# An int4 SwiGLU beside an S4 convolution on one core: each down-weight piece converted one group earlier, and the change of phase laid out anew

## Chip, cores and metric

One Trainium2 chip, one core. The metric is device time of one execution in microseconds (us), smaller is better.

## What is computed

The input is `u`, 2048 rows of 1024 numbers. The reference, cut to its core:

```python
xn = _layernorm(u)
K  = _s4_kernel(...)                       # 1024 taps, from a 64-state S4 system
y  = irfft(rfft(xn, 2L) * rfft(K, 2L))[:L] + D[0] * xn     # causal convolution along the row
Wg, Wu, Wd = dequantize(...)               # 4-bit words, (w - zero) * scale in groups of 64
h  = silu(xn @ Wg.T) * (xn @ Wu.T)         # 2752 columns
out = u + y + h @ Wd.T
```

## The kernel before, in words

Every large product runs with Strassen's scheme in Winograd's form: a 2 by 2 block product is done with seven smaller products (for x and h: A11, A12, S1 to S4, A22; for weights: B11, B21, B22, T1 to T4). Each factor is split into two float16 parts, a high part (rounded by ACT) and a low part (what is left, by GpSimd), and three of the four part products are taken. So each weight or hidden block goes through DVE (dequantize, sums), ACT (high part) and GpSimd (low part).

**Head (0 to 164 us).** x is read, normalized, and turned by TensorE into the stationary copies `xo[0]` and `xo[1]`, seven blocks each. Units 0 and 1 run beside it.

**Phase A.** 44 units; unit n is one tile of 128 hidden columns for gate and up on one half p of the rows, seven products of 12 matmuls in the order `TURN` (0, 3, 2, 1, 4, 5, 6). Between products ACT takes copies of the banks (`snap_s1`, `snap_s5`, `snap_u2`, `snap_u3`), on which the next products of the same unit wait (`products`, `snap_done`). Units 2 and 3 are written out; then the loop over groups g = 1 to 9 has units 4g to 4g+3. Unit 40 and the two short units 41 and 42 (64 columns left over, `tail_products`) end the phase with unit 43, which TensorE runs last.

In the same loop the down weight is prepared: piece g (`down_nibble`, `down_words`, `d_high`, `d_sum`, `d_low`) is 256 rows of it. In the kernel before, group g handles piece g-1, and its last four sums come in group g+1. Piece 8's sums lie beside unit 40, and piece 9 comes after the last, short piece 10, in the change of phase. Finished pieces are stored to `w_d` (`store_w`) from the slots `ds` and `ds_more`; hidden blocks are stored to `h_d` (`store_h`).

Words, scales and zeros of a weight tile come as a slab (`load_slab`, two slots `raw`/`sz`): 256 KB of words and 512 KB of scales and zeros. Slab m may be issued once slab m-2 is dequantized (`deq_done` at m-1).

**Phase B.** 56 down products, (sp_, j, s) in order, 33 matmuls each (`down`), with `wd[j]` (2816 KB each, read back from `w_d`) as moving and `hr` (704 KB for each product) as stationary data. DVE adds each to `acc`. 48 convolution pieces of 12 matmuls (`conv`) stand between them by the table `conv_pieces`; their strips come from two matmuls with `flip` after product (0, 0, 1), which need `kshift` from DRAM. The normalized x for them is stored to `xc_d` (8 blocks of 1024 KB, `store_xc`) and read back (`load_xc`).

**What sets the order.** Each engine's program is written out by hand. SP issues nearly all DMAs, and a wait in SP's program holds everything behind it. ACT issues only the first parts of `wd[0]`, `wd[1]` and `wd[2]` (`load_wd` in ACT's program, nine of eleven slices each); SP issues their rest and `wd[3]` to `wd[6]`. In the change of phase ACT's program has `load_wd(0)` behind `silu_tail(41)`, then the first half of piece 9 (`down_nibble(NG - 1, 0)`), `silu_tail(42)`, `load_wd(1)`, and `down_nibble(NG - 1, 1)` ahead of `snap_s1(43)`. A `down_nibble` waits for its slab.

## Time and profile before

| | us |
|---|---|
| three timed runs | 1496.56, 1498.66 (median), 1504.98 |
| the profiled execution | 1495.27 |
| its span in the trace | 1493.5 |
| TensorE busy in the span | 1333.8 (89%) |
| VectorE (DVE) / ScalarE (ACT) / GpSimd (POOL) busy | 957.6 / 457.3 / 674.7 |

The page gives busy time of each engine over the span. A stage view splits the span and shows which engine is full in which stage; a timeline gives for each instruction how long its engine sat idle before it, and who released it. Line numbers are those of the kernel before.

### The profile page before, as it was taken

The page shows a single profiled execution, that of the slowest core. Times are in us where ns is not written, and L with a number is a line of the kernel's source. Part 1 is how long each engine was busy: PE and PEld are TensorE (multiplying, and loading weights), DVE is VectorE, ACT ScalarE, POOL GpSimd, SP SyncE. Part 2 cuts the span into 40 slices and gives each one's busy share as a digit, 9 for nine tenths or more (in the row PEclk, how much of TensorE's full clock was granted, in tenths as well). Part 3 has the DMA queues.
Part 4 walks back from the last instruction along what each step waited for, and adds up shares of the span by engine and source line. Part 5 has one row for each costly group of instructions (what it writes and reads, how often), then busy time and mean ns, then how long its engine had stood idle before and what let it go on. Part 6 is the DMA issues. An engine that isn't in the chain of part 4 may idle for free. (4 is left out here: it accounts for less than half of the span.)

```text
span 1493.5 us, 17048 instructions
## 1 busy us (share of the span) xinstructions
PE 1333.8 (89%) x6299; PEld 630.9 (42%) x6299; DVE 957.6 (64%) x1057; ACT 457.3 (31%) x801; POOL 674.7 (45%) x484
## 2 busy tenths in 40 slices
PE   1557899988998999989999999449999999999998
PEld 1423444433443444434444444124444444444444
DVE  4744478899999898678898988535233332432341
ACT  3533444434444354444444543221000000000000
POOL 3642466766678688687978786341000000000000
PEclk9978999999999999999999999769999999999999
DMA  5301554343433344344444443779756236335431
GB/s 177 86 29 70 225 166 131 125 133 115 132 124 117 131 134 140 124 139 134 142 134 141 139 137 112 233 247 365 248 185 222 92 109 221 92 110 196 126 101 57
DMA packets 164646, 218.09 MB, mean 146 GB/s; under 512 B 41426, under 2 KB 121940, under 8 KB 162644
## 3 DMA queue, kind: packets, MB, share of 16 engines
q1 hardware_dynamic: 163988, 209.86, 42.8%
q10 hardware_dynamic: 576, 7.14, 1.4%
q8 instruction: 50, 0.82, 0.2%
q14 instruction: 32, 0.26, 0.1%
HBM read 139.64 MB, written 77.34 MB: 145 GB/s over the span
## 5 line engine op out<-in xcount | busy, mean ns | idle before, releaser
L1310 PE MATMUL px<-xo,wo 128*128 128x512 f16 x2016 | 473.9, 389 | 59.1 <-ACT py L960 30.2
L1310 PEld LDWEIGHTS px<-xo,wo 128*128 128x128 f16 x2016 | 200.1, 100 | 308.7 <-issue 26.5
L684 POOL TENSOR_TENSOR wo<-wf,wo 128x512 f16<-128x512 f32 x147 | 236.5, 1619 | 71.9 <-ACT wo L918 71.9
L703 POOL TENSOR_TENSOR hs<-hf,hs 128x512 f16<-128x512 f32 x154 | 210.8, 1375 | 103.2 <-ACT hs L953 96.1
L1394 PE MATMUL px<-wd,hr 128*128 128x512 f16 x1056 | 235.0, 382 | 10.7 <-DMA wd<-w_d 10.7
L1310 PE MATMUL pz<-xo,wo 128*128 128x512 f16 x1008 | 233.6, 382 | 0.0
L1394 PEld LDWEIGHTS px<-wd,hr 128*128 128x128 f16 x1056 | 102.6, 98 | 131.1 <-DMA wd<-w_d 11.2
L1310 PEld LDWEIGHTS pz<-xo,wo 128*128 128x128 f16 x1008 | 99.5, 99 | 120.8 <-issue 4.6
L1925 DVE SCALAR_TENSOR_TENSOR acc<-px,acc 128x512 f32<-128x512 f32 x32 | 22.1, 691 | 155.3 <-PE px L1394 151.3
L953 ACT ACTIVATE hs<-hf 128x512 f16<-128x512 f32 x154 | 94.5, 621 | 80.8 <-DVE hf L1569 48.2
L693 POOL TENSOR_TENSOR ds<-wf,ds 128x512 f16<-128x512 f32 x69 | 104.2, 1511 | 33.1 <-ACT ds_more L939 20.1
L1310 PE MATMUL py<-xo,wo 128*128 128x512 f16 x504 | 117.6, 384 | 0.0
L1479 DVE TENSOR_TENSOR wf<-wf,sz 128x1024 f32<-128x1024 int32 x63 | 113.4, 1800 | 5.7 <-ACT wf L893 3.8
L1394 PE MATMUL pz<-wd,hr 128*128 128x512 f16 x528 | 116.6, 379 | 0.0
L1480 DVE SCALAR_TENSOR_TENSOR wf<-wf,sz 128x1024 f32<-128x1024 f32 x63 | 112.6, 1788 | 2.2
L918 ACT ACTIVATE wo<-wf 128x512 f16<-128x512 f32 x147 | 90.8, 621 | 75.8 <-DVE wf L1480 55.4
L708 POOL TENSOR_TENSOR u<-u,s 128x512 f32<-128x512 f32 x42 | 60.6, 1442 | 56.7 <-ACT u L978 56.2
L1394 PEld LDWEIGHTS pz<-wd,hr 128*128 128x128 f16 x528 | 50.9, 98 | 58.6
L1310 PEld LDWEIGHTS py<-xo,wo 128*128 128x128 f16 x504 | 49.9, 99 | 60.7 <-issue 2.8
L1259 ACT ACTIVATE xc<-ctmp 128x512 f16<-128x512 f32 x8 | 5.0, 629 | 218.1 <-DVE ctmp L1950 218.1
L1477 DVE TENSOR_SCALAR wf<-raw 128x512 int32<-128x512 int32 x63 | 59.2, 939 | 17.4 <-DMA sz<-in_sz_down 12.8
L1264 ACT ACTIVATE us<-ctmp 128x512 f16<-128x512 f32 x16 | 10.1, 629 | 190.2 <-DVE ctmp L1970 190.2
(211 smaller groups left out, 1406.5 us busy)
## 6 DMA issues: line engine op xcount, KB each, us to landing
h_d<-hs SPq DMA_DIRECT2D x154, 256.0 KB, 3.7
hr<-h_d SPq DMA_DIRECT2D x56, 704.0 KB, 4.2
w_d<-ds SPq DMA_DIRECT2D x69, 256.0 KB, 3.9
wd<-w_d SPq DMA_DIRECT2D x4, 2816.0 KB, 12.5
sz<-in_sz_gate SPq DMA_DIRECT2D x21, 512.0 KB
sz<-in_sz_up SPq DMA_DIRECT2D x21, 512.0 KB
sz<-in_sz_down SPq DMA_DIRECT2D x20, 512.0 KB
xc_d<-xo SPq DMA_DIRECT2D x8, 1024.0 KB, 10.5
```

Source lines behind the costliest of these rows:

```text
L684: pool.tensor_tensor(w_dest(t, j, 1), w_place_of(j), w_dest(t, j, 0), ALU.subtract).then_inc(wlo_done, 1)
L693: pool.tensor_tensor(d_dest(q)[:, 1, :], d_place_of(g, j), d_dest(q)[:, 0, :], ALU.subtract)\
L703: pool.tensor_tensor(hs[:, j, :, 1, :], h_place_of(p, j), hs[:, j, :, 0, :], ALU.subtract)\
L708: pool.tensor_tensor(u3[:, :], u3[:, :], s5[:, :], ALU.add).then_inc(u2_done, 1)
L918: act.activation(w_dest(t, j, 0), w_place_of(j), ACT.Copy).then_inc(whi_done, 1)
L953: act.activation(hs[:, j, :, 0, :], h_place_of(p, j), ACT.Copy)\
L1310: done = pe.matmul(bank[:, :], wo[t % 2][:, j, wp, k * P:(k + 1) * P], xo[p][:, j, xp, k, :], start=(j in (0, 3) and k == 0 and wp == 0 an ...
L1394: done = pe.matmul(bank[:, :], hr[slot][:, k, hp, :], wd[j][:, k, wp, :], start=(OPENS[j] and k == 0 and hp == 0 and wp == 0), stop=(k == ...
L1477: link(dve.tensor_scalar(q[:, 1, :], r, 15, None, ALU.bitwise_and))
L1479: link(dve.tensor_tensor(w, q, sz[:, slot, 1:2, :].broadcast_to((P, 2, 512)), ALU.subtract))
L1480: dve.scalar_tensor_tensor(out=w, in0=w, scalar=WS, in1=sz[:, slot, 0:1, :].broadcast_to((P, 2, 512)), op0=ALU.mult, op1=ALU.mult).then_in ...
L1925: dve.scalar_tensor_tensor(out=part, in0=banks[BANK[j]][s][:, :], scalar=1.0 / (WS * HS), in1=part, op0=ALU.mult, op1=ALU.add).then_inc(ac ...
```

## The change

Five things are changed.

1. Piece g of the down weight is handled in group g, from `down_nibble(g, 0)` on; its last sums come in group g+1. Piece 0 stands in units 2 and 3, which had no piece. Piece 9's sums take piece 8's place beside unit 40, and only the short piece 10 is left in the change of phase. The slab numbers follow.
2. The eight stores of normalized x no longer stand together after the head; one of 1024 KB goes out in each of groups 1 to 8, after the slab of gate tile 2g+3.
3. ACT now issues `wd[0]` whole, `wd[1]` but for one slice, and `wd[2]`, `wd[3]`, `wd[4]` whole; the first two waits are for the stored pieces. SP issues one slice of `wd[1]`, then `wd[5]` and `wd[6]`.
4. `wd[2]` and `kshift` are placed in other parts of the buffer; `kshift` needs only the last tail slab dequantized.
5. In the first quarter of phase B the convolution pieces start after the sixth product instead of the fourth, and stand in pairs behind the last three.

The diff, cut to its core:

```diff
@@ places and tables
-    return 2 * t if t <= 2 else 6 * ((t - 1) // 2) + (0 if t % 2 else 3)
+    return 0 if t == 0 else 2 + 6 * ((t - 1) // 2) + (0 if t % 2 else 3)
 def slab_down(g, half):
-    return 65 + half if g == 9 else 6 * (g + 1) + 2 + 3 * half
+    return 6 * g + 4 + 3 * half
 def conv_pieces(sp_, i):
     if sp_ == 0:
-        return [] if i < 3 else [10, 11] if i == 13 else [i - 3]
+        return [] if i < 5 else [i - 5] if i < 11 else [2 * i - 16, 2 * i - 15]
-        w_place = [X0, X0 + 22 * K1, X0 + 56 * K1, X0 + 78 * K1, W0, W0 + 22 * K1, H0 + 20 * K1]
+        w_place = [X0, X0 + 22 * K1, W0, X0 + 56 * K1, X0 + 78 * K1, W0 + 22 * K1, H0 + 20 * K1]
@@ SP, behind the head
             load_x(7)
+            load_down(0, 0)
             load_gate(2)
+            sp.wait_ge(xlo_done, 56)
             load_up(2)
-            sp.wait_ge(xlo_done, 56)
-            for p in range(2):
-                for blk, kh, j in ((0, 0, A11), (0, 1, A12), (1, 0, S1), (1, 1, A22)):
-                    store_xc(p, blk, kh, j)
             store_h(0, 0, A11)
             store_h(0, 0, S3)
+            store_w(0, B11)
+            load_down(0, 1)
             for j in L_ORDER:
                 store_h(0, 0, j)
             load_gate(3)
-            load_up(3)
+            store_w(0, B21)
             for j in E_ORDER:
                 store_h(0, 1, j)
+            load_up(3)
+            store_w(0, B22)
@@ SP, group g
-                load_down(g - 1, 1)
-                store_w(g - 1, B21)
+                load_down(g, 1)
+                store_w(g, B21)
                 load_gate(2 * g + 3)
+                if g <= 8:
+                    store_xc(g - 1)
                 store_h(g, 1, S3)
@@ ACT, change of phase
             silu_tail(41)
-            load_wd(0)
+            load_wd(0, KC)
+            load_wd(1, KC - 1)
             h_high(NG, 0, S3)
...
-            down_nibble(NG - 1, 0)
             silu_tail(42)
-            load_wd(1)
-            d_high(NG - 1, B11)
             h_high(NG, 0, S1)
             h_high(NG, 0, S2)
-            down_nibble(NG - 1, 1)
             snap_s1(43)
-            d_high(NG - 1, B21)
...
             silu_first(43)
-            load_wd(2)
+            act.wait_ge(dlo_done, 7 * (NG + 1))
+            load_wd(2, KC)
+            load_wd(3, KC)
+            snap_u3(43)
+            silu_second(43)
+            load_wd(4, KC)
+            h_high(NG, 1, A12)
             h_high(NG, 1, A22)
-            snap_u3(43)
-            d_high(NG - 1, B22)
-            d_high(NG - 1, T1)
-            silu_second(43)
@@ DVE, units 1 to 3
             h_s3(0, 0)
+            down_words(0, 0)
             gate(2)
...
             t_sum(2, T4)
+            down_words(0, 1)
+            d_sum(0, T1)
+            d_sum(0, T3)
             h_first(3, 1, 1)
@@ DVE, group g
                 gate(2 * g + 1)
-                if g > 1:
-                    d_sum(g - 2, T2)
-                    d_sum(g - 2, T4)
+                d_sum(g - 1, T2)
+                d_sum(g - 1, T4)
```

How the order moves, at three places. **ACT, change of phase**, from the first nibble of piece 9 to the copy of unit 43's first bank (`py<-px`), before:

```order
L893 ACTIVATE wf<-raw,below 128x512 [waits slab_in1,dlo_done]
L1001 ACTIVATE g_61<-px 64x512 [waits hf_done,prod_done]
L1003 ACTIVATE sil<-py 64x512 [waits prod_done]
L995 DMA wd_80<-w_d 128x9216 [waits ds_out1]
L939 ACTIVATE ds<-wf 128x512 [waits ds_out0,deq_done]
L953 ACTIVATE hs<-hf_63 128x4x128 [waits hs_out3,hsum_done]
L953 ACTIVATE hs<-hf_63 128x4x128 [waits hs_out2,hsum_done]
L893 ACTIVATE wf<-raw,below 128x512 [waits slab_in0,dlo_done]
L960 ACTIVATE py<-px 128x512 [waits hf_done,prod_done]
```

and now, from the second short unit on:

```order
L975 ACTIVATE g_61<-px 64x512 [waits hf_done,prod_done]
L977 ACTIVATE sil<-py 64x512 [waits prod_done]
L926 ACTIVATE hs<-hf_63 128x4x128 [waits hs_out3,hsum_done]
L926 ACTIVATE hs<-hf_63 128x4x128 [waits hs_out2,hsum_done]
L933 ACTIVATE py<-px 128x512 [waits hf_done,prod_done]
```

The two conversions of nibbles (`wf<-raw,below`), which wait for a slab, and the high part between them are gone, and the load of `wd[1]` stands further ahead.

**ACT, a few instructions on**, from unit 43's `snap_u2` to the second silu; now:

```order
L945 ACTIVATE u_58<-px 128x512 [waits hf_done,prod_done]
L957 ACTIVATE g_61<-py 128x512 [waits hf_done,prod_done]
L969 DMA wd_81<-w_d 128x11264 [waits ds_out1,ds_out4,ds_out0,dlo_done]
L969 DMA wd_82<-w_d 128x11264 [waits ds_out3,ds_out0,ds_out1]
L951 ACTIVATE u_60<-px 128x512 [waits hf_done,prod_done]
L963 ACTIVATE sil<-px 128x512 [waits hf_done,prod_done]
L969 DMA wd_83<-w_d 128x11264 [waits ds_out5,ds_out0,ds_out1]
```

The loads of `wd[2]` and `wd[3]` stand between unit 43's first silu and its `snap_u3`, and each waits for stored pieces; before, one load (nine slices of `wd[2]`) stood there, and its wait was for piece 8 alone.

**DVE, units 3 and 4**, from unit 3's bank sum (`u_58<-pz`) to the first slab of unit 4's stretch, before:

```order
L1557 TENSOR_TENSOR u_58<-pz,u_58 128x512 [waits snap_done,prod_done]
L1530 TENSOR_TENSOR wf<-wf 128x2x256 [waits wsum_done]
L1569 SCALAR_TENSOR_TENSOR hf_64<-u_58,g_61 128x512 [waits u1_done,sil_done]
L1576 SCALAR_TENSOR_TENSOR hf_64<-u_60,sil 128x512 [waits u2_done,sil_done]
L1477 TENSOR_SCALAR wf<-raw 128x512 [waits slab_in0,wlo_done]
L1479 TENSOR_TENSOR wf<-wf,sz 128x1024 [waits nibble_done,dve_order]
L1480 SCALAR_TENSOR_TENSOR wf<-wf,sz 128x1024 [waits dve_order]
```

and now:

```order
L1529 TENSOR_TENSOR u_58<-pz,u_58 128x512 [waits snap_done,prod_done]
L1502 TENSOR_TENSOR wf<-wf 128x2x256 [waits wsum_done]
L1449 TENSOR_SCALAR wf<-raw 128x512 [waits slab_in1]
L1451 TENSOR_TENSOR wf<-wf,sz 128x1024 [waits nibble_done,dve_order]
L1452 SCALAR_TENSOR_TENSOR wf<-wf,sz 128x1024 [waits dve_order]
L1513 TENSOR_TENSOR wf<-wf 128x512 [waits dlo_done,deq_done]
L1517 TENSOR_TENSOR wf<-wf 128x512
L1541 SCALAR_TENSOR_TENSOR hf_64<-u_58,g_61 128x512 [waits u1_done,sil_done]
L1548 SCALAR_TENSOR_TENSOR hf_64<-u_60,sil 128x512 [waits u2_done,sil_done]
L1449 TENSOR_SCALAR wf<-raw 128x512 [waits slab_in0,wlo_done]
L1451 TENSOR_TENSOR wf<-wf,sz 128x1024 [waits nibble_done,dve_order]
L1452 SCALAR_TENSOR_TENSOR wf<-wf,sz 128x1024 [waits dve_order]
```

The second half of piece 0 (three instructions on a slab and two sums) has come in ahead of unit 3's hidden block. **SP, the same stretch**, before:

```order
L383 DMA h_d<-hs 128x4x256 [waits elo_done] x2
L383 DMA h_d<-hs 128x4x256 [waits llo_done] x5
L349 DMA raw<-in_raw_gate 128x512 [waits deq_done]
L350 DMA sz<-in_sz_gate 128x1x1024
L349 DMA raw<-in_raw_up 128x512 [waits deq_done]
L350 DMA sz<-in_sz_up 128x1x1024
L383 DMA h_d<-hs 128x4x256 [waits elo_done] x2
L383 DMA h_d<-hs 128x4x256 [waits llo_done]
L349 DMA raw<-in_raw_down 128x512 [waits deq_done]
```

and now:

```order
L382 DMA h_d<-hs 128x4x256 [waits elo_done] x2
L388 DMA w_d<-ds 128x1024 [waits dlo_done]
L348 DMA raw<-in_raw_down 128x512 [waits deq_done]
L349 DMA sz<-in_sz_down 128x1x1024
L382 DMA h_d<-hs 128x4x256 [waits llo_done] x5
L348 DMA raw<-in_raw_gate 128x512 [waits deq_done]
L349 DMA sz<-in_sz_gate 128x1x1024
L388 DMA w_d<-ds 128x1024 [waits dlo_done]
L382 DMA h_d<-hs 128x4x256 [waits elo_done] x2
L348 DMA raw<-in_raw_up 128x512 [waits deq_done]
L349 DMA sz<-in_sz_up 128x1x1024
L388 DMA w_d<-ds 128x1024 [waits dlo_done]
```

The slab of up tile 3 stood directly behind that of gate tile 3. It now stands behind a store of piece 0 and two of h, and its `deq_done` counts the second half of piece 0 too.

## Rows read from the trace of the kernel before

**Rows 1.** Windows by stage: us, busy (x count) of PE, PEld, DVE, ACT, POOL, PEclk, DMA share, GB/s
```profile
943.00:1025.40 82.40, 41.76 (x155) 17.02 (x156) 32.22 (x33) 23.55 (x41) 37.25 (x30) 0.75 0.80 274
1025.40:1488.30 462.90, 462.82 (x2358) 224.40 (x2356) 164.57 (x235) 16.51 (x26) 0.00 (x0) 1.00 0.47 156
```

**Rows 2.** Timeline of PE, 945 to 1025: start, length, instruction, [idle before <- releaser]
```profile
948.91 5.30 PE L1310 MATMUL px<-xo,wo 128*128 128x512 f16 x12 [6.01 <-DVE hf L1586]
...
979.34 4.19 PE L1310 MATMUL px<-xo,wo 128*128 128x512 f16 x12 [22.11 <-ACT py L960]
...
991.13 2.75 PE L1310 MATMUL px<-xo,wo 128*128 128x512 f16 x12
1004.55 16.87 PE L1394 MATMUL px<-wd,hr 128*128 128x512 f16 x66 [10.67 <-DMA wd<-w_d]
1023.38 1.98 PE L1435 MATMUL pv<-kshift,flip 128*128 128x512 f32 x4 [1.95 <-DMA kshift<-kpad]
```

**Rows 3.** Timeline of ACT, 940 to 1025
```profile
945.76 0.63 ACT L939 ACTIVATE ds<-wf 128x512 f16<-128x512 f32 x1 [13.36 <-DMA w_d<-ds]
...
957.17 0.63 ACT L939 ACTIVATE ds_more<-wf 128x512 f16<-128x512 f32 x1 [1.81 <-DVE wf L1549]
...
978.07 0.72 ACT L893 ACTIVATE wf<-raw,below 128x512 int32<-128x512 uint8 x1 [10.26 <-DMA sz<-in_sz_down]
978.70 0.58 ACT L960 ACTIVATE py<-px 128x512 f32<-128x512 f32 x1
```

**Rows 4.** DMA issues: the page's line for stored pieces; single issues near 963 and 986 us
```profile
w_d<-ds SPq DMA_DIRECT2D x69, 256.0 KB, 3.9
...
wd<-w_d ACTq DMA_DIRECT2D x1, 2304.0 KB, 12.5
...
w_d<-ds_more SPq DMA_DIRECT2D x1, 256.0 KB, 16.8
...
wd<-w_d ACTq DMA_DIRECT2D x1, 2304.0 KB, 9.3
```

**Rows 5.** DMA by queue (q10: ACT's), windows 968:972, 990:995, 996:1020: packets, MB, share
```profile
q10 hardware_dynamic: 78, 1.25, 83.4%
q1 hardware_dynamic: 189, 0.16, 12.5%
...
q10 hardware_dynamic: 92, 1.42, 81.7%
q1 hardware_dynamic: 229, 0.30, 16.2%
...
q1 hardware_dynamic: 4884, 9.18, 104.2%
```

**Rows 6.** Timeline of DVE, 100 to 230
```profile
168.22 0.42 DVE L1477 TENSOR_SCALAR wf<-raw 128x512 int32<-128x512 int32 x1
168.68 1.23 DVE L1479 TENSOR_TENSOR wf<-wf,sz 128x1024 f32<-128x1024 int32 x1
169.94 2.06 DVE L1480 SCALAR_TENSOR_TENSOR wf<-wf,sz 128x1024 f32<-128x1024 f32 x1
...
201.39 0.69 DVE L1569 SCALAR_TENSOR_TENSOR hf<-u,g 128x512 f32<-128x512 f32 x1
```

**Rows 7.** Timeline of ACT, 100 to 230
```profile
173.60 0.63 ACT L953 ACTIVATE hs<-hf 128x512 f16<-128x512 f32 x1 [3.24 <-DVE hf L1603]
...
206.41 0.72 ACT L893 ACTIVATE wf<-raw,below 128x512 int32<-128x512 uint8 x1 [0.47 <-DMA sz<-in_sz_up]
```

**Rows 8.** Timeline of PE, 60 to 260
```profile
194.79 2.76 PE L1310 MATMUL px<-xo,wo 128*128 128x512 f16 x12 [1.65 <-ACT u L972]
...
212.93 2.75 PE L1310 MATMUL px<-xo,wo 128*128 128x512 f16 x12
```

**Rows 9.** A slab load that ACT waits for: timelines of SP and ACT, 740 to 818
```profile
791.23 0.55 SPq L350 DMA_DIRECT2D sz<-in_sz_up  x1
...
799.92 0.72 ACT L893 ACTIVATE wf<-raw,below 128x512 int32<-128x512 uint8 x1 [5.18 <-DMA sz<-in_sz_up]
```

More of the change, by code:

```diff
@@ L197, in s4_plus_int4_swiglu @@
         ctmp = at("ctmp", [P, SB], f32, W0 + 56 * K1)
-        kshift = at("kshift", [P, 2, SB], f32, W0 + 52 * K1)
+        kshift = at("kshift", [P, 2, SB], f32, W0 + 24 * K1)
         strip = [at(f"strip{i}", [P, 2, SB], f16, (H0 + 16 * K1, H0 + 18 * K1, W0 + 58 * K1)[i]) for i in range(3)]
@@ L568, in store_out @@
                         .then_inc(out_done[s], 16)
-            store_w(NG - 1, B11)
             store_h(NG, 0, S1)
+            store_w(NG, T3)
             sp.wait_ge(prod_done, products_before(42))
             load_hr(0, 0, 0)
+            load_wd(1, KC - 1, KC)
             load_hr(0, 0, 1)
             store_h(NG, 0, S2)
-            store_w(NG - 1, B21)
+            store_w(NG, T4)
             store_h(NG, 0, S4)
             sp.dma_start(flip[:, :], flip_d).then_inc(flip_in, 16)
-            store_w(NG, T3)
-            load_wd(0, KC - 2, KC)
-            store_w(NG, T4)
-            store_h(NG, 1, A12)
-            store_h(NG, 1, A22)
-            store_w(NG - 1, B22)
-            store_w(NG - 1, T1)
-            load_wd(1, KC - 2, KC)
-            for j in (T2, T3, T4):
-                store_w(NG - 1, j)
+            sp.wait_ge(kpad_out, 48)
+            sp.wait_ge(deq_done, slab_tail(1, 1) + 1)
+            for n in range(2):
+                sp.dma_start(kshift[:, n, :], bass.AP(kpad.tensor, n * (P + L // 2) + 1, [[1, P], [1, SB]]))\
+                    .then_inc(kshift_in, 16)
             sp.wait_ge(prod_done, PHASE_A)
@@ L1247, in _ @@
             act.wait_ge(kscale_done, 1)
+            for i in range(2, 6):
+                q = max(q for q in SPLIT_TURN if split_slot(q) == i)
+                act.wait_ge(ds_out[i], 16 * (SPLIT_TURN[q] + 1))
             scale = ksc[:, 0:1].bitcast(f32)
@@ L1849, in _ @@
                 h_s4(g - 1, 1)
-                down_words(g - 1, 0)
+                down_words(g, 0)
                 h_s3(g, 0)
@@ L1868, in _ @@
                 t_sum(2 * g + 2, T4)
-                down_words(g - 1, 1)
+                down_words(g, 1)
                 h_s12(g, 0)
-                d_sum(g - 1, T1)
-                d_sum(g - 1, T3)
+                d_sum(g, T1)
+                d_sum(g, T3)
                 h_s4(g, 0)
@@ L1897, in _ @@
                 d_sum(NG, j)
-            down_words(NG - 1, 0)
             h_s12(NG, 0)
@@ L1901, in _ @@
             h_s4(NG, 0)
-            down_words(NG - 1, 1)
-            for j in T_ORDER:
-                d_sum(NG - 1, j)
             c12(43)
```

175 lines of the change are left out of this document (73 added, 102 removed).

## The prediction

> **What bounds the kernel now.** First the stages. From 1025.4 us on TensorE is busy 462.82 of 462.90 us [rows 1]: phase B is full, so the moment at which its second kind of product (j = 1) starts sets the end, one for one. From 943 to 1025.4, the change of phase, it is busy 41.76 of 82.40, at a granted clock of 0.75, with the DMA engines at 0.80. The time is lost here. TensorE's timeline [rows 2] splits it: 6.01 us for the short unit's hidden block, 22.11 for ACT's copy of unit 43's first bank, 10.67 for `wd[0]`, 1.95 for `kshift`. ACT's timeline [rows 3] says why the copy is late: at 978.07 it ends a wait of 10.26 us for a slab of piece 9, and the copy follows at 978.70. The slab in turn travels beside ACT's own load of `wd[1]`, which took 12.5 us, while a store of 256 KB beside it took 16.8 instead of the usual 3.9 [rows 4]. While ACT's queue (q10) is at work it takes 83.4% and 81.7% of the engines, SP's queue (q1) 12.5% and 16.2%; in MB per us that is 0.31 and 0.28 against 0.04 and 0.06. Alone, q1 moves 9.18 MB in 24 us, 0.383 [rows 5]. Everything below hangs on this.
>
> **Part 1, piece 0 in units 2 and 3.** The work per group is the same afterwards; only its place moves, so what counts is the stretch that had no piece. Three steps.
>
> (a) `down_words(0, 0)` stands ahead of `gate(2)`. A slab costs DVE 0.42 + 1.23 + 2.06 = 3.7 us there [rows 6]. ACT already waits 3.24 us for the sum behind it (173.60), and has the copy that TensorE wants behind that [rows 7], so nothing hides it: 3.5 us, bounds 2.9 (two ops at 1.23) and 5.5 (all in their longer form).
>
> (b) The eight stores of x leave this stretch. Stores of h then land sooner, and part of the 1.65 us wait at 194.79 [rows 8] goes: I give back 0.7, bounds 0 and 1.65.
>
> (c) The slab of up tile 3 may now be issued only when the second half of piece 0 is dequantized. Unit 3's hidden block was at 201.39 [rows 6]; DVE takes up the half piece about there plus the 2.8 us of (a) and (b), and is through at about 207. A slab load that ACT waits for was issued at 791.23 and let ACT go at 799.92, 8.7 us [rows 9]. So the slab is there at 216, where ACT asks for it at 206.41 [rows 7] plus 2.8. ACT then has seven instructions of some 0.6 us up to the copy for the product that ran at 212.93 [rows 8]: it is ready at about 220 instead of 215.7. 4.3 us, bounds 0 (a load of 4 us) and 6.
>
> Sum of part 1: +7 us, bounds +3 and +11. DVE catches up in groups 1 and 2, since it still waits for TensorE there; but TensorE is behind by these 7 us, and phase A has nothing to give them back.
>
> **Part 2, stores of x one per group.** 1024 KB at 0.383 MB per us is 2.7 us of the engines, eight times. The store is issued behind the gate slab and well ahead of the next up slab. I take 0. If that cover were gone, it is the last rival below.
>
> **Part 3, change of phase.** Up to 945.76 nothing changes: ACT still waits for the store of the last full piece [rows 3]. Then:
>
> - ACT holds at `load_wd(0)` until the piece just made is stored: made by 948, landed 3.9 us later [rows 4], so the load goes out at about 952, six us later than now, but with `wd[1]` on its heels. ACT had idle time behind this place, so the hold costs its chain 1 or 2 us.
> - The last high part ahead of the second short unit was at 957.17 [rows 3]. Behind it stand two silus and two h parts, no slab. With the hold I put the copy of unit 43's bank at 962 to 963 instead of 978.70. TensorE goes on at about 963 instead of 979.34, and its five products, which took from 979.34 to 993.88 [rows 2] (the first at 4.19 us, after the long idle time at the lower clock, then 2.75), end at about 977.5. By this alone phase B would begin 16 us earlier, and if `wd[0]` and `hr` were there, 27.
> - Are they? ACT now issues 2816 + 2560 + 3 x 2816 KB = 14.2 MB. SP must bring to the start of j = 1: thirteen stores of 256 KB, four `hr` of 704 KB, the slice of `wd[1]`, `flip` and `kshift`, together 7.1 MB. The first two loads run from 954 to about 974. `load_wd(2)` waits for a store that sits in SP's queue: it lands once q10 is empty, and I allow 5 us for this gap, in which q1 moves 1.9 MB. Then q10 has 8.7 MB more, ahead of `hr`. At 0.28 MB per us, the lower of [rows 5], q10 is busy 50.5 us in all and ends at 954 + 50.5 + 5 = 1009.5. By then q1 has moved 50.5 x 0.05 + 1.9 = 4.4 of its 7.1 MB; the rest takes 2.7 / 0.383 = 7.1 us. So j = 1 starts at 1016.6 instead of 1023.38 + 1.98 = 1025.36 [rows 2]: -8.8 us.
> - Meanwhile ACT holds `snap_u3(43)` and the last silu behind `load_wd(2)`, some 3 us of waiting for TensorE's last product. It is free, since `hr` is later.
>
> Bounds of part 3. If SP's queue were never starved, TensorE's own path rules: 977.5, the first pair of products 16.87, the flips 1.98, so 996.4, or -29. If q10 runs all the way as its second load did, 2304 KB in 12.5 us, 0.189 MB per us [rows 4], the same sum gives 954 + 75 + 5 = 1034 and j = 1 at about 1038: +13.
>
> **Part 4, convolution pieces.** The same twelve pieces in the first quarter, later, and in pairs at its end. DVE's work between pieces is the same; I take 0, bounds 0 and +3.
>
> **Sum.** +7 - 8.8 = -1.8 us against the profiled execution's 1495.27: 1493.5. The median of the runs lies 3.4 us above that execution, which would make it 1496.9. I give **1495**. This is a forecast of no change: a measurement of this kernel tells about 0.5%, 7.5 us, from nothing. The 41 us of waits go, but most of them turn into waits for data that the DMA engines can't bring sooner.
>
> **Rivals.**
>
> *The queues share better than the rows show.* For it: at 968 us q1's packets were small (189 for 0.16 MB), at 990 too, while `hr` is read in rows of 704 KB / 128 = 5.5 KB. Against it: at 990:995 two `hr` loads were already under way, and q1 moved 0.30 MB. At an even split of 0.34 MB per us the 5.0 MB that SP has left after 976 take 29.4 us, so j = 1 starts at 1005.5: -20 + 7 = -13, **1482**; down to TensorE's own path, -29 + 7 = -22, 1473. The Trainium skill ("DMA: Bandwidth & Descriptors", section "Issuing engines are not separate DMA queues") says that DMAs of several engines run on the same 16 DMA engines and interleave, so that the issuer matters for little but the sequencer's time; by that rule alone ACT's loads would take nothing from SP's, and this rival would hold. [Rows 5] speak against it, and the same page ("Queues, rings and completion order") has the turns go by packet, which favours the queue with the long rows.
>
> *ACT's loads run slower, and the end comes later.* Place: q10 from 952 on, with SP's stores and `hr` beside it. For it: the second load's 12.5 us against 9.3 for the third [rows 4]. It decides from a mean rate of q10 below about 0.225 MB per us: then j = 1 starts at 954 + 63 + 5 + 4 = 1026, no gain is left, and part 1's 7 us stand. With the first pair at 0.189 and the rest at 0.28 it gives **1502**, at 0.189 throughout 1515. Against it: slabs of piece 9, which travelled beside that second load, are gone.
>
> *The stores of x delay slabs in each group.* ACT already waits 5.18 us for a slab once in a group [rows 9], so a slab is no cheap thing. Price: 8 x 2.7 = 22 us, **1515**. Against it: that slab is issued ahead of the store, and the one behind it only after three more stores of h.
>
> *Nothing moves where it counts*: part 1 is hidden and part 3 gives back what it gains, 1495.
>
> **How the numbers follow.** Forecast 0.44 (own range 1484 to 1503: 0.10 faster, 0.32 the same, 0.02 slower). Better sharing 0.30, faster. Slower loads 0.12 and late slabs 0.06, slower. Nothing moves 0.08, the same. Faster 0.40, same 0.40, slower 0.20. The range 1478 to 1506 takes in the forecast, most of the first rival and the near end of the second. The forecast's and the rivals' shares are close; the likeliest single case is no change.
>
> **What would show it.** In the new profile: the wait of 22.11 us gone and TensorE back at about 963 plus 7; then, between the last product of unit 43 and the flips, waits for `hr<-h_d` and `kshift` of 20 us or more in all, with q10 above 70% of the engines; j = 1 at about 1016.6 + 7 = 1024. In the head, TensorE waiting 4 us for ACT's copy of unit 2 (L945) and again in unit 4, with ACT waiting about 7 for `sz<-in_sz_up`. I am wrong if q1 carries `hr` at over 0.1 MB per us beside q10, if `wd[2]` goes out much later than 976, or if unit 4 begins no later than now.

## The result, and the profile after

| | before | after |
|---|---|---|
| median of 16 runs each, side by side (us) | 1499.32 | 1490.40 |
| lowest to highest | 1496.56 to 1504.98 | 1486.26 to 1495.99 |
| profiled execution / its span | 1495.27 / 1493.5 | 1489.69 / 1487.9 |
| first short unit (41) starts | 922.02 | 935.66 |
| j = 1 of phase B starts | 1025.20 | 1019.04 |

The ratio of the runs is 0.994, interval 0.9927 to 0.9952: the change makes the kernel 0.6% faster, just past the 0.5% that the prediction named as the limit of no change. Behind this small number stand two large ones. Phase A ends 13.6 us later, the change of phase is 19.8 us shorter (83.38 us from unit 41 to j = 1, against 103.18), and phase B is what it was. For these stages one profiled execution of each kernel is compared with one. Unit 41's start moves by nearly 8 us between executions of kernels that are alike up to there (931.5 to 939.2, in after and six of the runs below), so the 13.6 is uncertain by several microseconds. The stretch from unit 41 to j = 1 moves far less: 82.8 to 83.8 us in after and the four runs that leave its order alone (copies_first, start4, xc_head, conv_before).

Two stage windows of after, the change of phase behind the two short units, and phase B (columns as in [rows 1]):

```profile
956.60:1019.00 62.40, 40.73 (x154) 16.96 (x155) 22.37 (x21) 18.25 (x32) 28.52 (x23) 0.79 0.93 365
1019.00:1482.00 463.00, 463.00 (x2354) 224.31 (x2353) 165.74 (x236) 16.56 (x26) 0.00 (x0) 1.00 0.46 148
```

TensorE's work in the change of phase is the same 41 us, now in 62.4 us instead of 82.4 [rows 1], at a clock of 0.79 of full, and the DMA engines are at 0.93 instead of 0.80. TensorE's timeline of after in this stage:

```profile
962.22 4.32 PE L1282 MATMUL px<-xo,wo 128*128 128x512 f16 x12 [5.67 <-DVE hf L1558]
...
976.51 5.30 PE L1282 MATMUL px<-xo,wo 128*128 128x512 f16 x12 [7.38 <-ACT py L933]
...
989.80 2.75 PE L1282 MATMUL px<-xo,wo 128*128 128x512 f16 x12
992.39 14.41 PE L1366 MATMUL px<-wd,hr 128*128 128x512 f16 x66
...
1015.47 3.78 PE L1407 MATMUL pv<-kshift,flip 128*128 128x512 f32 x4 [8.66 <-DMA kshift<-kpad]
```

Of [rows 2], the wait of 22.11 us for ACT's copy is now 7.38, the one of 10.67 for `wd[0]` is gone, and the one of 1.95 for `kshift` is 8.66. No product waited for `hr`. ACT's timeline of after shows what stands ahead of the copy now that no slab does:

```profile
959.06 0.63 ACT L912 ACTIVATE ds<-wf 128x512 f16<-128x512 f32 x1 [12.99 <-DMA w_d<-ds]
...
960.24 0.59 ACT L975 ACTIVATE g<-px 64x512 f32<-64x512 f32 x1
...
975.87 0.58 ACT L933 ACTIVATE py<-px 128x512 f32<-128x512 f32 x1
```

ACT waits 12.99 us for the store of the slot into which it wants to put a down block (13.36 in [rows 3]), and the silu of the short unit goes out at 960.24, behind that wait. Counted from the start of unit 41 the copy comes 40.2 us later; before, it came after 56.7. And SP's timeline of after shows what `kshift` stood behind:

```profile
983.38 0.45 SPq L535 DMA_DIRECT2D hr<-h_d  x1
...
985.67 8.80 SPq L573 DMA_DIRECT2D flip<-in_flip  x1
994.57 12.78 SPq L577 DMA_DIRECT2D kshift<-kpad  x2
```

The loads of `hr` went out at 982 to 983, before ACT's next loads at 985.50; `flip` and `kshift` came behind them, and the issuing itself took 8.80 and 12.78 us. In the 20 us from 990 on the two queues moved (packets, MB, share of the 16 engines):

```profile
q10 hardware_dynamic: 396, 8.20, 95.4%
q1 hardware_dynamic: 397, 0.38, 5.4%
```

The same number of packets, and 22 times the bytes: one of q10's holds 20.7 KB, one of q1's 1 KB. The packets are as even inside ACT's loads of before. The queues of before, 968 to 971 and 992 to 994:

```profile
q10 hardware_dynamic: 58, 1.07, 94.2%
q1 hardware_dynamic: 59, 0.08, 7.4%
...
q10 hardware_dynamic: 31, 0.57, 96.5%
q1 hardware_dynamic: 32, 0.07, 8.4%
```

The windows of [rows 5], 968 to 972 and 990 to 995, take in one microsecond more, in which ACT's load runs out and q1 has 130 and 197 packets. That is where their 2.4 packets of q1 to one of q10 come from. (At the start of the first of these loads, 965 to 968, q1 was ahead as well, 72 packets to 36; why is open.)

The start lost more than forecast. TensorE's timeline of after, units 2 to 4 and the first wait for the resolvent, which in before ended at 303.17:

```profile
179.51 4.83 PE L1282 MATMUL px<-xo,wo 128*128 128x512 f16 x12 [4.78 <-ACT u L945]
...
201.21 2.76 PE L1282 MATMUL px<-xo,wo 128*128 128x512 f16 x12 [1.33 <-ACT u L945]
...
225.70 5.28 PE L1282 MATMUL px<-xo,wo 128*128 128x512 f16 x12 [6.18 <-ACT u L945]
230.77 3.14 PE L1282 MATMUL pz<-xo,wo 128*128 128x512 f16 x12
...
318.81 0.60 PE L1307 MATMUL pv<-vw,s4w 128*128 128x8 f32 x2 [4.61 <-DVE s4w L1641]
```

and ACT's wait in front of the second of these, in ACT's timeline of after:

```profile
221.26 0.72 ACT L866 ACTIVATE wf<-raw,below 128x512 int32<-128x512 uint8 x1 [7.29 <-DMA sz<-in_sz_up]
```

The products behind the two waits ran 4.83 and 5.28 us instead of 2.75: at 1.2 instead of 2.4 GHz for most of their length (the granted clock from 165 to 185 us is 0.83, and 1.00 in before), and TensorE had idled 4.78 and 6.18 us right before. From the resolvent's first wait to unit 41 after takes 616.9 us and before 618.9, and kernels alike in this stretch take 615.4 to 621.3: what the start lost, 15.6 us here, does not come back by an amount that can be told from the spread. The stores of x in the loop cost nothing that shows: the last three waits of the loop are 1.59, 1.63 and 1.68 us, before 1.40, 1.42 and 2.00.

### The profile page after: what moved, and what is told of

Its sections match the earlier page's. It is cut to its first block and busy times, and to the rows that moved or that the text cites. A ratio compares the mean times of both kernels' runs of the same rounds, so it can differ in the third digit from the quotient of the medians.

```text
span 1487.9 us, 17049 instructions
## 1 busy us (share of the span) xinstructions
PE 1337.9 (90%) x6299; PEld 631.8 (42%) x6299; DVE 964.6 (65%) x1057; ACT 457.6 (31%) x801; POOL 676.2 (45%) x484
## 5 line engine op out<-in xcount | busy, mean ns | idle before, releaser
L1282 PE MATMUL px<-xo,wo 128*128 128x512 f16 x2016 | 479.1, 392 | 50.8 <-ACT u L945 32.1
L674 POOL TENSOR_TENSOR ds<-wf,ds 128x512 f16<-128x512 f32 x73 | 109.7, 1502 | 11.9 <-ACT ds L912 11.9
L689 POOL TENSOR_TENSOR u<-u,s 128x512 f32<-128x512 f32 x42 | 62.1, 1478 | 50.8 <-ACT u L951 50.0
L1548 DVE SCALAR_TENSOR_TENSOR hf<-u,sil 128x512 f32<-128x512 f32 x42 | 43.7, 1039 | 41.6 <-ACT sil L963 30.7
```

Of the source, the lines that this page charges most:

```text
L674: pool.tensor_tensor(d_dest(q)[:, 1, :], d_place_of(g, j), d_dest(q)[:, 0, :], ALU.subtract)\
L689: pool.tensor_tensor(u3[:, :], u3[:, :], s5[:, :], ALU.add).then_inc(u2_done, 1)
L1282: done = pe.matmul(bank[:, :], wo[t % 2][:, j, wp, k * P:(k + 1) * P], xo[p][:, j, xp, k, :], start=(j in (0, 3) and k == 0 and wp == 0 an ...
L1548: dve.scalar_tensor_tensor(out=hf[p][:, t % 2, 1, :], in0=u3[:, :], scalar=HS / (XS * WS), in1=sil[:, :], op0=ALU.mult, op1=ALU.mult).then ...
```

## The experiments

Theory A: the start and unit 43 lose time because ScalarE runs its program in order, and a copy that frees a bank of TensorE stands behind a wait of another kind. Theory D: in the change of phase ACT's queue starves SP's while it has work. Against A stands that VectorE has too much to do in units 2 to 8 whatever the order; against D, that SP's own order (theory C) or the bytes as a whole decide. Of the twelve runs below five came inside a range that was stated for them (copies_first in its rival's, tails_first, act_late2, conv_before, start4 in its rival's) and best3 in the one for a wait that only moves; the other six did not, and what each misses is said with it. Medians, and ratios to the runs of before beside them:

| kernel | us | ratio (interval) | unit 41 | j = 1 | between |
|---|---|---|---|---|---|
| copies_first | 1487.28 | 0.9914 (0.9895 to 0.9933) | 933.69 | 1016.83 | 83.1 |
| kshift_first | 1490.92 | 0.9940 (0.9924 to 0.9956) | 937.37 | 1020.17 | 82.8 |
| act_late | 1493.93 | 0.9960 (0.9945 to 0.9975) | 937.04 | 1023.79 | 86.8 |
| tails_first | 1490.91 | 0.9935 (0.9917 to 0.9953) | 931.47 | 1016.50 | 85.0 |
| act_late2 | 1482.37 | 0.9900 (0.9877 to 0.9924) | 939.19 | 1010.86 | 71.7 |
| xc_head | 1499.48 | 1.0017 (1.0002 to 1.0033) | 946.99 | 1029.78 | 82.8 |
| conv_before | 1491.00 | 0.9954 (0.9938 to 0.9970) | 938.27 | 1022.04 | 83.8 |
| best2 | 1481.28 | 0.9885 (0.9859 to 0.9911) | 934.15 | 1001.00 | 66.9 |
| small_rows | 1499.02 | 0.9993 (0.9980 to 1.0007) | 934.89 | 1027.88 | 93.0 |
| best3 | 1478.45 | 0.9853 (0.9835 to 0.9871) | 932.46 | 1004.98 | 72.5 |
| start4 | 1485.53 | 0.9907 (0.9893 to 0.9922) | 933.02 | 1016.14 | 83.1 |
| best4 | 1480.91 | 0.9883 (0.9870 to 0.9896) | 929.15 | 996.40 | 67.3 |

### The start: copies_first, start4

```
 ScalarE, unit 2                    ScalarE, unit 4 (group 1)
+snap_u2(2)                        +snap_s5(4); snap_u2(4); silu_first(4)
 h_high(0, 0, S1)                   up_nibble(3)
-snap_u2(2)                         ...
```

> ScalarE copies TensorE's banks (snap_u2 of unit 2; snap_s5, snap_u2 and silu_first of unit 4) ahead of the instructions that wait for piece 0 of the down weight, instead of behind them. Theory A (the start loses its time because ScalarE runs in order: a copy that frees a bank stands behind a wait for VectorE or for a slab): TensorE's waits of 4.78 us at 179.5 and 6.18 us at 225.7 fall to under 1 us each, the slow products behind them (4.83 and 5.28 + 3.14 us instead of 2.75 each) go back to 2.75, and unit 41 starts 12 to 15 us earlier, at 921 to 924 instead of 935.66. Of this 9 to 15 us arrive at the end: 1475 to 1482 us, about 1476. Rival B (engines and slabs are simply too late for piece 0 there, whatever the order of the copies): the waits move to other products of units 2 to 5 and unit 41 starts at 932 or later, 1487 to 1491 us.

TensorE's timeline of copies_first:

```profile
179.14 5.34 PE L1288 MATMUL px<-xo,wo 128*128 128x512 f16 x24 [0.20 <-ACT u L951]
...
250.01 4.89 PE L1288 MATMUL px<-xo,wo 128*128 128x512 f16 x12 [6.36 <-ACT py L933]
...
311.32 0.59 PE L1313 MATMUL pv<-vw,s4w 128*128 128x8 f32 x2 [4.62 <-DVE s4w L1647]
```

Both waits are gone, with their slow products, and the first wait for the resolvent ends 7.5 us earlier than in after (4 to 7.5 us earlier than in the seven executions with the order of after, 315.48 to 318.83). But a wait of 6.36 us has come up in unit 6, where ACT waits 7.36 us for the first hidden block of unit 5, which VectorE makes after the numerators. Theory A named the right two places and the wrong total: 1487.28, not 1476. By its numbers the rival came true: the wait moved (one unit further than it said), unit 41 at 933.69, 1487 to 1491. The interval of the ratio overlaps that of the change (0.9927 to 0.9952), so a gain is likely and not shown. start4 follows the wait: the copies of unit 6 first as well, and the numerators one unit later (`if n == 6: numerators()`).

> The start alone, the change of phase as in the change. The bank copies of units 2, 4 and 6 stand ahead of the waits for slabs and for h, and VectorE makes the numerators one unit later. Theory A: no wait of over 2 us between 170 and 300 (after: 4.78 and 6.18; copies_first: 6.36 in unit 6; best3: 6.98 in unit 6), the resolvent's first wait ends at 303 to 307 instead of 318.8, unit 41 starts at 924 to 930: 1479 to 1486 us, about 1482. Rival (VectorE's work bounds units 2 to 8, so that a wait only moves): the wait shows again in unit 7 or 8 and the resolvent's first wait ends at 310 or later: 1485 to 1489 us.

TensorE's timeline of start4, and ACT's at the same place:

```profile
268.51 5.30 PE L1297 MATMUL px<-xo,wo 128*128 128x512 f16 x12 [6.57 <-ACT py L933]
...
312.34 0.59 PE L1322 MATMUL pv<-vw,s4w 128*128 128x8 f32 x2 [4.62 <-DVE s4w L1656]
```

```profile
266.82 0.63 ACT L926 ACTIVATE hs<-hf 128x512 f16<-128x512 f32 x1 [5.12 <-DVE hf L1556]
...
267.88 0.58 ACT L933 ACTIVATE py<-px 128x512 f32<-128x512 f32 x1
```

The wait has moved on to unit 7 at the same size, and the resolvent's wait ends at 312.34, no better: the rival holds. The runs further down bear it out with other orders: one wait of 6.61 us in unit 6 and an end at 314.80 in best2, 6.98 and 313.30 in best3, and, with start4's order once more, 6.58 and 313.94 in best4. The window from 165 us to that wait, in before:

```profile
165.00:303.20 138.20, 131.48 (x609) 59.11 (x607) 107.28 (x120) 63.33 (x114) 92.59 (x67) 1.00 0.51 176
```

in after:

```profile
165.00:318.80 153.80, 136.90 (x610) 60.36 (x607) 120.33 (x131) 68.13 (x124) 103.10 (x74) 0.95 0.41 133
```

and in start4:

```profile
165.00:312.30 147.30, 133.12 (x601) 58.95 (x599) 123.50 (x128) 66.63 (x120) 108.70 (x74) 0.97 0.43 139
```

Up to the same point of the program VectorE has 13.1 us more to do in after (120.33 against 107.28) and 16.2 in start4; its share goes from 78% to 84%. The seven executions with the start of after end the resolvent's wait at 317.7 us in the mean, the five with another order at 313.1, before at 303.2. So of some 14.5 us at the start about 4.5 are ACT's order and its price in clock. The other 10 stayed in all four orders that were tried beside that of the change (8 to 12 us), and are put down to the piece itself on VectorE. That any order would lose them was not shown, nor was the piece's work taken away from this stretch alone.

### The stores of x, and the table of pieces: xc_head, conv_before

```
 SP: +for i in range(8): store_xc(i)   ahead of store_h(0, 0, A11)
     -if g <= 8: store_xc(g - 1)       in the loop
```

> The eight stores of xc go back to their old place ahead of the first h stores (all at about 166), none in the loop. By the prediction's part 2 (worth nothing): 1488 to 1492 us, the waits before units of the loop unchanged at 1.6 us. Rival (the xc stores in the loop delay slabs): phase A shortens by 3 us or more after unit 8, 1486 or less. Rival (at the head they delay the slabs of piece 0 and tile 3 further, since they fill the queue for about 22 us): the waits in units 2 to 4 grow by 3 to 8 us, 1492 to 1498 us; this one is the likeliest, at about 1493.

TensorE's and SP's timelines of xc_head:

```profile
207.75 5.30 PE L1282 MATMUL px<-xo,wo 128*128 128x512 f16 x12 [8.59 <-ACT u L945]
...
234.16 4.44 PE L1282 MATMUL px<-xo,wo 128*128 128x512 f16 x12 [5.14 <-ACT u L945]
```

```profile
173.27 7.77 SPq L393 DMA_DIRECT2D xc_d<-xo  x8
...
190.58 7.92 SPq L388 DMA_DIRECT2D w_d<-ds  x1
198.54 1.01 SPq L348 DMA_DIRECT2D raw<-in_raw_down  x1
```

1499.48 us, a ratio of 1.0017 against 0.9940: taken back alone, this move costs 0.8%, all that the change gains and a little more. With eight MB in the queue the slab of piece 0's second half goes out at 198.54 instead of 191.67, and an `hs` slot comes free late (ACT waits 9.88 us for `h_d<-hs` at 202.42); unit 3 waits 8.59 us instead of 1.33. The change of phase is as in after. The time lies just above even the 1492 to 1498 of the likeliest rival. The stores can't stay where they stood in the head once piece 0 is there; another place in the head was not tried.

conv_before takes back the table: `return [] if i < 3 else [10, 11] if i == 13 else [i - 3]`.

> The pieces of the convolution of the first quarter of phase B stand where they stood before (one from j=1 on). By the prediction's part 4 (worth 0 to 3 us): 1489 to 1493 us. Rival (the gain of the change of phase hangs on the later start of the pieces, since strips and xc(0,0) are not there at j=1): TensorE waits at the first piece, at about 1034, for strip or xc, 4 us or more: 1494 to 1500 us. Rival (the late pieces cost): 1487 or less.

1491.00, with no wait at a piece: the intervals of the two overlap. Phase B from j = 1 to the end of the span is 468.7 us against 468.9. The table is worth nothing that can be measured.

### The change of phase: kshift_first, act_late, act_late2, small_rows, tails_first

kshift_first moves `flip` and `kshift` in SP's program ahead of `load_hr(0, 0, 0)`.

> SP issues flip and kshift ahead of the loads of hr(0,0) instead of four instructions behind them, so that they go out at about 982, in the gap between ScalarE's loads of wd. Theory C (kshift alone was late: it was issued behind flip when ScalarE's queue was full again, the rest of SP's loads had time): TensorE's wait of 8.66 us at 1015.5 goes, the flips run at full clock, and j=1 starts 9 to 11 us earlier, at about 1009: 1479 to 1482 us. Theory D (ScalarE's queue starves SP's, whatever stands first in it): kshift lands at about 985, but hr(0,1,0) and hr(0,1,1), which SP issues once unit 43 is done at about 993, land only when ScalarE's queue is empty at about 1010 to 1013; j=1 starts at 1012 to 1016, 3 to 7 us earlier: 1484 to 1488 us. Rival E (the wait is for DMA bytes as a whole): j=1 as now, 1489 us.

TensorE's timeline of kshift_first:

```profile
993.68 7.28 PE L1366 MATMUL px<-wd,hr 128*128 128x512 f16 x33 [0.59 <-issue]
1009.47 9.15 PE L1366 MATMUL px<-wd,hr 128*128 128x512 f16 x33 [8.51 <-issue]
1018.46 1.88 PE L1407 MATMUL pv<-kshift,flip 128*128 128x512 f32 x4
```

`kshift` landed 5 us after its issue and nobody waits for it. In its place the second half of j = 0 waits 8.51 us: `hr(0, 0, 1)`, now issued at 985.80, is caught behind ACT's loads. No gain (82.8 us against 83.4). Whatever stands last in SP's program when q10 wakes up is the one that is late. Theory C falls. D named the wrong victim (`hr(0, 1)`) and 1484 to 1488 us; the time is nearer to rival E's 1489 (the bytes as a whole), and this run does not tell the two apart.

act_late leaves SP alone and lets ACT wait:

```
 load_wd(2, KC)
-load_wd(3, KC)
 snap_u3(43); silu_second(43)
-load_wd(4, KC)
+act.wait_ge(kshift_in, 32); act.wait_ge(hr_in[3], 16)
+load_wd(3, KC); load_wd(4, KC)
```

> SP's order is untouched. ScalarE issues wd[3] and wd[4] only when kshift and hr(0,1,1) have landed, instead of at 985.5 and 992.7. Theory D (ScalarE's queue takes 94 to 97 per cent of the DMA engines while it has work and leaves SP's queue 4 to 6): its queue is empty at about 991 to 993 after wd[2], kshift lands by about 999 and hr(0,1) by about 1003, TensorE goes from j=0 through the flips without a wait and j=1 starts at 1009 to 1011: 1480 to 1482 us. Theory C (the place in SP's order is what delays kshift) and a rival in which the total of bytes decides: kshift still lands after 1010 and j=1 starts at 1015 or later, 1486 to 1490 us. If wd[3] or wd[4] are late now, TensorE waits at j=3 or j=4 (about 1040 or 1054), which would give the gain back.

Slower, 1493.93, for a reason of my own making. TensorE's timeline of act_late, then ACT's:

```profile
1013.58 8.66 PE L1368 MATMUL px<-wd,hr 128*128 128x512 f16 x33 [13.62 <-DVE hf L1550]
```

```profile
1007.59 1.67 ACT L926 ACTIVATE hs<-hf 128x512 f16<-128x512 f32 x3 [14.12 <-DMA hr<-h_d]
```

`kshift`'s two halves landed 5.2 and 6.4 us after their issues at 995.3 and 996.8, by about 1003 instead of 1015. But the wait stood ahead of ACT's last splits of h; GpSimd's low parts, then its u, then VectorE's last hidden block hung on them, and TensorE on that. act_late2 puts five of the seven splits first.

> As act_late, but ScalarE makes its first five splits of h of unit 43 before it waits for kshift and hr(0,1,1), so that the wait holds up nobody (in act_late its wait held the splits, GpSimd behind them, u, and with it the last hf: TensorE waited 13.62 us at 1013.6 for hf). SP's order is untouched. Theory D (ScalarE's queue starves SP's): kshift lands near 1002 as in act_late, TensorE goes through j=0 at 992 to 1007 without a wait and j=1 starts at 1008 to 1012, 7 to 11 us earlier than after: 1479 to 1484 us. Rival (total bytes, or SP's order): kshift lands after 1010, 1487 to 1491 us. Rival G (the loads held back are missed): waits for wd at j=3 or j=4 at about 1038 or 1053, 1487 us or more.

TensorE's timeline of act_late2:

```profile
994.90 14.41 PE L1370 MATMUL px<-wd,hr 128*128 128x512 f16 x66
...
1009.14 1.88 PE L1411 MATMUL pv<-kshift,flip 128*128 128x512 f32 x4
```

No wait, the flips at full clock, 71.7 us instead of 83.4 from unit 41 to j = 1, and 1482.37 us, in spite of a late phase A in the profiled execution. Same bytes, same order on SP, two loads later: theory D holds, and the total of bytes (rival E) does not decide. `wd[3]` and `wd[4]` were not missed (no wait over 0.8 us behind 1010).

small_rows asks what in ACT's queue does it. `wd[3]` and `wd[4]` go out in eleven transfers each, slice by slice (`step = 1 if j in (3, 4) else k1`), so that a row is 2 KB; `snap_u3(43)` was also moved ahead of `load_wd(3)`.

> SP's order and the moment of ScalarE's loads are those of the change; only wd[3] and wd[4] are loaded in eleven transfers each, with rows of 2 KB in place of 22 KB. Theory H (the two queues take turns packet by packet: in stretches in which both have work the trace of the change counts as many packets of the one as of the other, 93 and 93, 106 and 104, but 2.1 MB against 0.1 MB, since a packet of ScalarE's queue holds 22 KB and one of SP's 0.5 to 5.6 KB): from about 993 on SP's queue gets 20 to 60 per cent of the bytes instead of 5, kshift lands by about 1003 instead of 1015, hr(0,1) by about 1006, and j=1 starts at 1008 to 1013: 1480 to 1485 us. Rival I (a queue with more bytes waiting, or ScalarE's queue as such, is served first, whatever its packets): shares stay at 94 to 5 and j=1 starts at 1015 or later, 1487 to 1491 us. Risk: 22 issues of a third of a microsecond hold ScalarE's copies of unit 43 by 4 to 7 us, which would show as waits on ScalarE at 988 to 993.

The queues of small_rows from 1000 to 1005 us:

```profile
q10 hardware_dynamic: 701, 1.28, 66.3%
q1 hardware_dynamic: 708, 0.73, 40.9%
```

Again one packet for one, and now q1 gets 36% of the bytes (0.73 of 2.01 MB) instead of 4%; `kshift`'s halves landed 10.6 and 13 us after their issues at 994.5 and 995.3, by about 1008 and not 1015. Theory H holds for the shares. Its time does not: 1499.02. ACT's timeline of small_rows shows the risk that was named, larger than named:

```profile
986.43 9.86 ACTq L971 DMA_DIRECT2D wd<-w_d  x11
996.39 0.60 ACT L963 ACTIVATE sil<-px 128x512 f32<-128x512 f32 x1 [9.45 <-issue]
996.50 14.16 ACTq L971 DMA_DIRECT2D wd<-w_d  x11
```

The 22 issues took 24 us, where a single one of ACT's took 0.33 (985.21 in this run). The last splits of h stood behind them, as in act_late, and TensorE waited 18.15 us.

tails_first moves, on ACT, `silu_tail(41)`, `silu_tail(42)` and `snap_s1(43)` ahead of the splits of the down weight that wait for stores, and `snap_s5(43)`, `snap_u2(43)` ahead of those that wait for sums.

> In the change of phase ScalarE takes the silus of the short units 41 and 42 and the copies of unit 43 ahead of the splits of piece 9, which wait for stores. Theory A (ScalarE's order makes TensorE wait) and theory D (the DMA queues bound the end of the stage) together: the waits of 5.67 us at 962 and 7.38 us at 976.5 shrink to under 2 us each and unit 43 ends at 975 to 979 instead of 992.4, but TensorE then waits for hr(0,0) until about 984 to 987 and for kshift until about 1015 as now: j=1 at 1017 to 1021, 1487 to 1491 us, no gain. Rival F (what TensorE loses in unit 43 is lost for good): j=1 starts 9 to 13 us earlier, 1477 to 1481 us.

TensorE's timeline of tails_first, and ACT's:

```profile
964.65 2.76 PE L1281 MATMUL px<-xo,wo 128*128 128x512 f16 x12 [1.94 <-ACT u L945]
...
983.66 4.86 PE L1281 MATMUL px<-xo,wo 128*128 128x512 f16 x12 [13.65 <-ACT u L951]
...
1012.93 3.78 PE L1406 MATMUL pv<-kshift,flip 128*128 128x512 f32 x4 [10.16 <-DMA kshift<-kpad]
```

```profile
983.01 0.60 ACT L951 ACTIVATE u<-px 128x512 f32<-128x512 f32 x1 [5.75 <-issue]
```

The two waits are gone, and one of 13.65 us stands in their place: ACT holds its `snap_u3(43)` behind `load_wd(2)`, which waits for a store. Behind that `kshift` is late as ever. 85.0 us instead of 83.4: no gain, and 1490.91 lies in the range that A and D together gave, but not by their way: unit 43 was to end at 975 to 979 and TensorE then to wait for `hr`, and it is unit 43 itself that waited. So this run does not show what a unit 43 without waits is worth (the profiled execution's early j = 1 is its early phase A).

### Together: best2, best3, best4

best2 has copies_first, `gate(2)` ahead of piece 0 on VectorE, the numerators later; in the change of phase the order of tails_first with all copies of unit 43 ahead of the loads, `kshift` behind `hr(0, 0, 1)`, `wd[1]` held until `hr(0, 0, 1)` has landed and `wd[2]` to `wd[4]` until `kshift` and `hr(0, 1, 1)` have, and some smaller moves with them (SP's slab of gate tile 2, VectorE's `h_tail(42, 1)`, GpSimd's `c22(43)`).

> All that the first four runs suggest together. Start: the bank copies first; gate(2) and the first sums of h ahead of piece 0 on VectorE, which idled 8.15 us right after; the numerators of the resolvent one unit later. Change of phase: silus of the short units and the copies of unit 43 ahead of the splits, h of unit 42 ahead of the sums of piece 9, kshift behind hr(0,0,1), and ScalarE loads wd[1] only when hr(0,0,1) and wd[2..4] only when kshift and hr(0,1,1) have landed. Theories A and D together: unit 41 starts at 922 to 928, unit 43 runs without waits, TensorE waits once for hr(0,0) up to 15 us, j=1 starts at 992 to 1002 instead of 1019: 1462 to 1474 us, about 1467. If only the start holds: about 1480. If only the change of phase holds: about 1474. Rival (bytes of DMA bound the change of phase whatever the order): j=1 at 1010 or later, 1480 us or more.

1481.28, where 1462 to 1474 was expected. Unit 43 runs without a wait, j = 1 starts at 1001.00, but j = 2 then waits 4.56 us for `wd[2]` and 2.92 more behind it: held too long. The start kept a wait of 6.61 us. best3 takes the start of copies_first again, with the first copy of unit 6 early, and loads `wd[2]` right behind `wd[1]`, `wd[3]` when `hr(0, 2, 1)` has landed and `wd[4]` when `hr(0, 3, 1)` has.

> As best2, with three differences. Start: as copies_first (VectorE's order is that of the change, the numerators stay in unit 5), and the first copy of unit 6 stands ahead of the split of h that waited 7.36 us for VectorE at 248.75 in copies_first. Change of phase: ScalarE loads wd[2] right behind wd[1], wd[3] when hr(0,2,1) has landed, and wd[4] when hr(0,3,1) has. Theories A and D: the start has no wait of over 2 us before 300, unit 41 starts at 924 to 930; j=1 starts at 992 to 1002 and no product of j=2 and j=3 waits over 2 us (4.56 and 2.92 us in best2): 1466 to 1475 us, about 1470. If the start's wait only moves on again (VectorE's work is what bounds units 2 to 8): 1474 to 1480 us.

1478.45, 1.5% faster than before, and 0.9% faster than the change by the two ratios. j = 1 waits 4.74 us, nothing after it; the start's wait is 6.98 us in unit 6. best4 joins start4's start to it and holds `wd[2]` until `hr(0, 1, 1)` has landed.

> The start of start4 and the change of phase of best3, with wd[2] loaded when hr(0,1,1) has landed instead of right behind wd[1], and the last two splits of h behind the load of wd[3]. Theory D: TensorE waits for hr(0,0) and wd[1] as in best3 (9.6 us), goes through j=0 and the flips, and no product of j=1 to j=4 waits over 2 us (best2: 4.56 and 2.92 at j=2; best3: 4.74 at j=1); j=1 starts at 992 to 1001. With the start at 924 to 930: 1466 to 1475 us, about 1471. If the start's wait only moves: 1473 to 1478 us.

TensorE's timeline of best4:

```profile
978.48 16.37 PE L1387 MATMUL px<-wd,hr 128*128 128x512 f16 x66 [9.69 <-issue]
...
1027.72 7.30 PE L1387 MATMUL pz<-wd,hr 128*128 128x512 f16 x33 [1.04 <-DMA wd<-w_d]
...
1049.69 8.97 PE L1387 MATMUL px<-wd,hr 128*128 128x512 f16 x33 [4.29 <-issue]
```

j = 1 starts at 996.40, as said, but the first product of j = 4 waits 4.29 us, and the median misses both ranges (1466 to 1475, and 1473 to 1478 if the start's wait only moves). The profiled execution was the fastest of its six runs (1473.91, median 1480.91), so its rows flatter it. best3 has the lowest median of this study; that it beats best4 rests on runs on two chips, each against its own runs of before, on four runs of best3, and the two intervals touch. How much of the gain of these three is the start and how much the change of phase was not taken apart.

## Why the prediction was right, and where it was wrong

1495 was forecast and 1490.4 measured, inside the range; the likeliest case, "no change", was missed by a little. The two terms of the sum had the right sign and were each too small, and their errors (some 6.6 and 11 us) went against each other. That the sum came out nearer than either term is luck. The two profiled executions differ by 5.6 us, the medians by 8.9; the rest is the spread between executions.

**Part 1, +7 us, measured +13.6 (+15.6 at the first wait for the resolvent).** The mechanisms and places were right: TensorE waited for ACT's copy in unit 2 (4.78 us) and in unit 4 (6.18), with ACT waiting 7.29 for the slab of the up tile, where "about 7" was said. By terms: (a) 3.5 forecast, the wait in unit 2 grew by 4.3; (b) -0.7 forecast, -0.3; (c) 4.3 forecast, 6.18. That is 10.2 of waits. Missing was a term: behind each wait the products run at the low clock, 2.1 us in unit 2 and 2.9 in unit 4 (5.28 + 3.14 against twice 2.75). [Rows 2] had shown exactly this (4.19 and 5.30 us for a product behind a wait), and I used it in part 3 and not in part 1. "DVE catches up in groups 1 and 2" was wrong too: start4 and the three runs with best in their name show that taking the waits away only moves one on, with VectorE busy for 84% of the stretch in start4.

**Part 2, nothing: right for the loop, wrong for the head.** In the loop the stores cost nothing. But what the move gives was put down as 0.7 us in (b), and xc_head shows 0.8% by the ratios, some 11 us. The step read a wait of 1.65 us and put it down to the stores, and didn't ask what they would do to a slab that has to pass the same queue now. This is no error of the sum (the stores did move), but of its reasons.

**Part 3, -8.8 us, measured -19.8.** The places, counted from the start of unit 41 so that part 1's error drops out:

| | forecast | after |
|---|---|---|
| ACT's copy of unit 43's first bank | 40.5 | 40.2 |
| ACT's first load of `wd` is issued | 30.0 | 27.4 |
| from there until q10 is through with its 14.2 MB | 57.5 | 47 |
| from there to j = 1 | 7.1 | 9 |
| j = 1 | 94.6 | 83.4 |

- *ACT's copy at 962 to 963*: right, to 0.3 us. It came at 975.87 only because phase A ended 13.6 us later. The wait for the stored piece was kept as it was (13.36, now 12.99), and the hold at `load_wd(0)` is 2.67 us, where 1 or 2 was said.
- *q10 at 0.28 MB per us*: this is the term that was mis-sized, and nearly all of the error. The windows of [rows 5] from which it was taken take in the end of ACT's load: in 990 to 995 all but 0.02 MB had gone by 994. In the midst of its loads q10 moved 0.36 MB per us in before from 968 to 971, and 0.33 from 987 to 994 (2.34 MB in 7 us). At 0.34 the 14.2 MB take 42 us, not 50.5, and the same sum gives -17. In after q10 moved 0.40 from 965 to 977 (4.82 MB in 12 us) and 0.41 from 990 to 1010; its packets hold 20 KB there and 18 KB in before, which goes some of the way and was not tested by itself. The Trainium skill ("DMA: Bandwidth & Descriptors", "Queues, rings and completion order") has the turns go by packet; the trace agrees in after (396 to 397) and in before (58 to 59), and small_rows shows it as a cause. The Trainium skill's section "Issuing engines are not separate DMA queues" on the same page, by which the issuer matters for little, says nothing of shares: what counted here was how long the rows of either queue were.
- *A gap of 5 us in which q1 moves 1.9 MB*: right (1.90 MB from 980 to 985).
- *`hr` late*: wrong. The first two `hr` went out in that gap, so TensorE could do all of j = 0 while q10 worked, and only `kshift` and `hr(0, 1)` came late. This moved no term of the sum, which counted only when SP's last bytes for j = 1 land.

**Part 4, nothing: right.** From j = 1 to the end of the span it is 468.9 us, before 468.3, and conv_before has 468.7 with the old table.

**The rivals.** "The queues share better" had the right price for the change of phase (-20 us) and the wrong mechanism: q1 got 4% of the bytes beside q10, where [rows 5] have 11% and 17% (7% and 11% in the stretches inside the loads). "TensorE's own path", -29 us and 74.4 us from unit 41 to j = 1, was given as the bound if SP's queue were never starved; with the loads held and ACT's order changed as well, best2 and best4 take 66.9 and 67.3. "ACT's loads slower" and "stores of x delay slabs" did not occur. **What would show it**: unit 2, unit 4 and q10 above 70% came as said; waits of 20 us for `hr` and `kshift` did not (8.66 for `kshift` alone), nor j = 1 at 1024 (1019.04). Of "what would make it wrong" nothing came: q1 carried 0.02 MB per us beside q10, and `wd[2]` went out at 985.50, which is 49.8 us after unit 41's start where 976 meant 54.

Open: what the start would cost in the best order for VectorE, and how the early piece would do if its first half came one unit later; neither was tried. The terms (a) to (c) of part 1 were read off one execution; no run takes one of them back by itself.
